# A grouped-query layer whose four input products run in three float32r passes, and whose turned rows are split by ScalarE and VectorE

## The reference

```python
q = x @ Wq                       # 256 -> 256
k = x @ Wk                       # 256 -> 64: four groups of heads share keys
v = x @ Wv                       # 256 -> 64
q = _rope(q, cos, sin); k = _rope(k, cosk, sink)
p = softmax(q @ k.T / sqrt(D));  o = (p @ v) @ Wo
# feed-forward on the same x, 64 slots
ctx = concatenate([x, slot_mean])
h = gelu(ctx @ w1.T + b1)
route_logits = (h @ w2.T + b2) / (abs(tau) + 0.1)
# top 8 of 64, softmax: alpha; slot_input = alpha.T @ x; a GRU step; out = alpha @ slot_values
```

## Time and profile before

| what | value |
|---|---|
| median of 3 runs | 3073.55 us (3070.24 to 3075.05) |
| profiled execution | 3092.09 us, span 3090.4 us |
| mean granted clock of TensorE | 0.956 of full speed |
| PEld (weight loads) | 1805.8 us, 58% |
| ACT (ScalarE) | 1387.8 us, 45% |
| POOL (GpSimd) | 394.5 us, 13% |

### The profile page before, as it was taken

The page is one execution under the profiler, slowest core; times in us unless marked ns, Lnnn a source line. Parts: engine busy times, 40 slices in busy tenths (PEclk is TensorE's granted clock), DMA queues, the critical chain, the costliest instruction groups (busy, mean ns, idle before and its releaser), DMA issues.

```text
span 3090.4 us, 53706 instructions
## 1 busy us (share of the span) xinstructions
PE 2780.4 (90%) x15686; PEld 1805.8 (58%) x15687; DVE 1868.2 (60%) x4512; ACT 1387.8 (45%) x2011; POOL 394.5 (13%) x373
## 2 busy tenths in 40 slices
PE   4999999999988888888879999999899579999998
PEld 2566556546644444443437777776666356666666
DVE  5666666666637777777737677772122456566653
ACT  1644554454433555555545455432233144444443
POOL 1011001100100000000021211221111312222220
PEclk7999999999987999999999999999999789999999
DMA  6534543654412122221214111122311233333330
GB/s 193 166 119 139 171 140 104 180 152 138 119 39 88 56 70 70 70 69 56 70 51 166 46 36 54 48 89 71 109 62 60 89 98 105 103 102 102 101 98 16
DMA packets 157951, 294.55 MB, mean 95 GB/s; under 512 B 24928, under 2 KB 82657, under 8 KB 149057
## 3 DMA queue, kind: packets, MB, share of 16 engines
q1 hardware_dynamic: 145264, 259.59, 27.8%
q0 software_dynamic: 10464, 28.59, 3.0%
q10 hardware_dynamic: 2160, 5.61, 0.5%
HBM read 194.02 MB, written 99.68 MB: 95 GB/s over the span
## 4 chain that ended last, share of the span: by engine, by line
PE 69%; DVE 12%; DMA 6%; issue 6%; ACT 4%; SPq 2%; DVEq 0%; another core or an unknown queue 0%; POOL 0%; ACTq 0%; POOLq 0%
PE bank_u L573 6%; PE pair L557 5%; PE pair L616 4%; PE bank L1984 4%; PE pair L733 4%; PE pair L2134 4%; DVE nmax L910 3%; PE pair L3074 3%; PE pair L777 3%; PE bank_m L3038 3%; PE bank L534 3%; PE bank L3038 3%; PE bank L2589 3%; PE pair L1482 2%; DMA k_a<-parts_dram 2%
## 5 line engine op out<-in xcount | busy, mean ns | idle before, releaser
L816 ACT ACTIVATE probs<-pair 128x1024 f32<-128x1024 f32 x512 | 502.1, 1021 | 218.7 <-PE pair L557 217.9
L910 DVE TENSOR_REDUCE nmax<-bank 128x1 f32<-128x512 f32 x664 | 441.8, 685 | 175.1 <-PE bank L534 127.0
L910 DVE TENSOR_REDUCE nmax<-bank_m 128x1 f32<-128x512 f32 x360 | 246.5, 685 | 106.7 <-PE bank_m L534 59.8
L573 PE MATMUL bank_u<-probs,vext 128*32 128x512 f32 x2048 | 288.7, 637 | 0.6 <-ACT uraw L803 0.5
L557 PE MATMUL pair<-q_a,k_a 98*128 98x512 f32 x512 | 176.4, 450 | 22.2 <-ACT probs L816 11.8
L534 PE MATMUL bank<-k_a,q_a 96*128 96x512 f32 x336 | 149.3, 479 | 27.4 <-DMA k_a<-parts_dram 24.0
L2282 DVE CUSTOM_DVE_ANT_0 bank<-bank,mask_q 128x128 f32<-128x128 f32 (+1 forms) x320 | 118.8, 420 | 89.5 <-PE bank_m L2024 67.1
L557 PEld LDWEIGHTS pair<-q_a,k_a 98*128 98x128 f32 x512 | 90.3, 202 | 122.0 <-ACT probs L816 66.4
L797 ACT ACTIVATE mrow<-bank 8x512 f32<-8x512 f32 x87 | 50.2, 577 | 231.1 <-PE bank L543 231.1
L2134 PE MATMUL pair<-fc,hid 128*128 128x256 f32 x512 | 133.2, 399 | 6.3 <-ACT probs L2175 6.3
L1455 PE MATMUL bank<-k,q 62*128 62x512 f32 x302 | 113.2, 478 | 26.7 <-DVE nmax L910 26.7
(11 more groups left out here) (471 smaller groups left out, 6036.9 us busy)
## 6 DMA issues: line engine op xcount, KB each, us to landing
parts_dram<-parts SPq DMA_DIRECT2D x64, 512.0 KB
q<-parts_dram SPq DMA_DIRECT2D x126, 128.0 KB
q_a<-parts_dram SPq DMA_DIRECT2D x31, 512.0 KB
k_a<-parts_dram SPq DMA_DIRECT2D x31, 512.0 KB
xs<-xres SPq DMA_DIRECT2D x24, 512.0 KB, 3.1
xl<-xs SPq DMA_DIRECT2D x24, 512.0 KB, 3.9
x_in<-xg SPq DMA_DIRECT2D x74, 128.0 KB, 2.1
yg_dram<-y_out POOLq DMA_DIRECT2D x72, 128.0 KB, 2.0
```

The costliest lines, as they stand in the source:

```text
L573: ins = nc.tensor.matmul(bank_u[32 * h:32 * h + 32, :], vext[:, kt, kv(g, h), :], probs[:, kt % 2, h * SEQ:(h + 1) * SEQ], start=(kt == 0) ...
L816: nc.scalar.activation(probs[:, kt % 2, hp * 2 * SEQ:hp * 2 * SEQ + n], st.tile(l, name)[:, 0:n], ACT.Exp).then_inc(st.free["act"].sem, 1)
L910: nc.vector.tensor_reduce(nmax[:, g % 2, qt, h:h + 1], sc.tile(l, name)[:], AX, ALU.max, negate=True).then_inc(sc.free["dve"].sem, 1)
```

## The change

1. The four weights of the products, Wq, Wk, w1's part for x and Wv, are split once into a high and a low part, by GpSimd behind POST0 (`pool_split1`: four copies, four subtractions). TensorE waits for the eight instructions ahead of PRE1.
2. ScalarE's copy of T becomes `act_turned_high` into `xnT_high1`, in the same place. VectorE gets `dve_turned_low`, which subtracts it from T and so frees T; in the plan T's reader is now VectorE. It stands behind maximum 13 of group 2 and before 14.
3. `project` takes three float32r passes of two feature blocks, six matmuls a half; the first two passes wait for the high part, the third for the low one. `pe_values` is replaced by `values`, with 24 matmuls of 64 columns.
4. Buffers: `xnT_high1` and the split weights are new; the whole weights lie where the low parts and others do in turn; `spare_q` shrinks. GpSimd waits for V of POST1 before it splits weights for a later layer.

```diff
 def st_plan1(front, back):
-    return parts_of(front, back, ("back", [("V", "dve")] + e_uses(0, 0, 2)), ("front", [("T", "act")]),
+    return parts_of(front, back, ("back", [("V", "dve")] + e_uses(0, 0, 2)), ("front", [("T", "dve")]),
...
-        turned_high = sig("turned_high", [(1, 0), 0, 0, 0], "scalar")
+        turned_high = sig("turned_high", [(1, 0), (1, 0), 0, 0], "scalar")
...
-        def act_turned_high(act, l, it):
+        def act_turned_high(act, l, it, high):
             act.wait_ge(*st.filled(l, it, "T"))
-            nc.scalar.activation(xnT_high0[:, :, :].rearrange("p k n -> p (k n)").bitcast(F32R), st.tile(l, "T")[:],
+            nc.scalar.activation(high[:, :, :].rearrange("p k n -> p (k n)").bitcast(F32R), st.tile(l, "T")[:],
                                  ACT.Copy).then_inc(turned_high.sem, 1)
...
+        def dve_turned_low(dve, l, it, high):
+            dve.wait_ge(*turned_high.at(l, it, 1))
+            nc.vector.tensor_tensor(xnT_low[:, :, :].rearrange("p k n -> p (k n)").bitcast(F32R), st.tile(l, "T")[:],
+                                    high[:, :, :].rearrange("p k n -> p (k n)"), ALU.subtract).then_inc(st.free["dve"].sem, 1)
...
-            def project(name, half, weight, width=P, halves=2):
+            def project(name, half, high, low, width=P, halves=2, before_low=lambda: None):
...
-                for k_ in range(KT):
-                    ins = nc.tensor.matmul(st.tile(l, name)[0:width, half * SEQ:(half + 1) * SEQ], weight[:, k_, :], xnT[:, k_, :],
-                                           start=(k_ == 0), stop=(k_ == KT - 1))
+                for n, (weight, turned) in enumerate(((high, xnT_high1), (low, xnT_high1), (high, xnT_low))):
+                    if n == 2:
+                        before_low()
+                    for k_ in range(KT):
+                        ins = nc.tensor.matmul(st.tile(l, name)[0:width, half * SEQ:(half + 1) * SEQ],
+                                               weight[:, k_, :].bitcast(F32R), turned[:, k_, :].bitcast(F32R),
+                                               start=(n == 0 and k_ == 0), stop=(n == 2 and k_ == KT - 1))
...
-                pe_values(pe, l, it, wv1)
+                values()
...
+            def values():
+                for s in st.vacated(l, it, "V"):
+                    pe.wait_ge(*s)
+                for t in range(TT):
+                    at = slice(t * P, (t + 1) * P)
+                    for n, (turned, weight) in enumerate(((xnT_high1, wv1_high), (xnT_high1, wv1_low), (xnT_low, wv1_high))):
+                        for k_ in range(KT):
+                            ins = nc.tensor.matmul(st.tile(l, "V")[:, t * DIM:t * DIM + 64], turned[:, k_, at].bitcast(F32R),
+                                                   weight[:, k_, :].bitcast(F32R),
+                                                   start=(n == 0 and k_ == 0), stop=(n == 2 and k_ == KT - 1))
+                ins.then_inc(st.full.sem, 1)
...
+            def turned_parts():
+                pe.wait_ge(*done(st, l, it, "T"))
...
                 if front and g == 0:
-                    pe.wait_ge(*done(st, l, it, "T"))
-                    project("QQ", 0, wq1[:, :, 0:P])
+                    pe.wait_ge(*turned_high.at(l, it, 1))
+                    project("QQ", 0, wq1_high[:, :, 0:P], wq1_low[:, :, 0:P], before_low=turned_parts)
...
                     if front and g == 0 and kt == 1:
-                        act_copy_xnT(act, l, it)
+                        act_turned_high(act, l, it, xnT_high1)
...
-                maxima(2, 10, 16)
+                maxima(2, 10, 14)
+            if front:
+                dve_turned_low(dve, l, it, xnT_high1)
             if back:
+                maxima(2, 14, 16)
                 maxima(3, 0, 2)
...
+        def pool_split1(pool):
+            parts1 = ((wq1, wq1_high, wq1_low), (wk1, wk1_high, wk1_low), (w1x, w1x_high, w1x_low), (wv1, wv1_high, wv1_low))
+            pool.wait_ge(loaded1, N1)
+            pool.wait_ge(*st.filled(POST0, 0, ("E", GROUPS - 1, TT - 1, 1)))
+            for w, high, low in parts1:
+                nc.gpsimd.tensor_copy(high[:].bitcast(F32R), w[:]).then_inc(weights1_split, 1)
+            pool.wait_ge(weights1_split, 4)
+            for w, high, low in parts1:
+                nc.gpsimd.tensor_tensor(low[:].bitcast(F32R), w[:], high[:], ALU.subtract).then_inc(weights1_split, 1)
...
             pool0(pool, POST0, 0, step)
+            pool_split1(pool)
...
             pool1(pool, POST1, 0, step)
+            pool.wait_ge(*st.filled(POST1, 0, "V"))
             pool_split_weights(pool)
...
             pe.wait_ge(dve_set1, 5)
+            pe.wait_ge(weights1_split, 8)
             pe1(pe, PRE1, 0)
```

More of the change, by code:

```diff
@@ L843, in early @@
                 if kt == 2 and front:
-                    act_turned_high(act, l, it)
+                    act_turned_high(act, l, it, xnT_high0)
             def first_max(kt):
@@ L976, in dve0 @@
             if front:
-                dve.wait_ge(*turned_high.at(l, it, 1))
-                nc.vector.tensor_tensor(xnT_low[:, :, :].rearrange("p k n -> p (k n)").bitcast(F32R), st.tile(l, "T")[:],
-                                        xnT_high0[:, :, :].rearrange("p k n -> p (k n)"), ALU.subtract).then_inc(st.free["dve"].sem, 1)
+                dve_turned_low(dve, l, it, xnT_high0)
             maxima(3, 6, 12)
@@ L1263, in build @@
         q_1 = sb("q_1", [P, GROUPS, GH // 2, SEQ], F32, l1)
-        spare_q = sb("spare_q", [P, 8 * SEQ], F32, l1)
+        xnT_high1 = sb("xnT_high1", [P, KT, SEQ], F32, l1)
+        wq1_high = sb("wq1_high", [P, KT, DIM], F32, l1)
+        wk1_high = sb("wk1_high", [P, KT, 2, 64], F32, l1)
+        w1x_high = sb("w1x_high", [P, KT, P], F32, l1)
+        wv1_high = sb("wv1_high", [P, KT, 64], F32, l1)
+        spare_q = sb("spare_q", [P, 1920], F32, l1)
         k_1 = sb("k_1", [P, GROUPS, SEQ], F32, l1)
@@ L1277, in build @@
         sin1 = sb("sin1", [P, SEQ], F32, l1)
-        wq1 = sb("wq1", [P, KT, DIM], F32, l1)
+        whole_wq1 = ExitStack()
+        wq1 = sb("wq1", [P, KT, DIM], F32, whole_wq1)
+        whole_wq1.close()
+        wq1_low = sb("wq1_low", [P, KT, DIM], F32, l1)
         wos = sb("wos", [P, KT, DIM], F32, l1)
@@ L1282, in build @@
         turn_k = sb("turn_k", [64, 2, SEQ], F32, l1)
-        w1x = sb("w1x", [P, KT, P], F32, l1)
+        whole_w1x = ExitStack()
+        w1x = sb("w1x", [P, KT, P], F32, whole_w1x)
+        whole_w1x.close()
+        w1x_low = sb("w1x_low", [P, KT, P], F32, l1)
         w1s = sb("w1s", [P, KT, P], F32, l1)
-        wk1 = sb("wk1", [P, KT, 2, 64], F32, l1)
-        wv1 = sb("wv1", [P, KT, 64], F32, l1)
+        whole_wk1 = ExitStack()
+        wk1 = sb("wk1", [P, KT, 2, 64], F32, whole_wk1)
+        whole_wk1.close()
+        wk1_low = sb("wk1_low", [P, KT, 2, 64], F32, l1)
+        whole_wv1 = ExitStack()
+        wv1 = sb("wv1", [P, KT, 64], F32, whole_wv1)
+        whole_wv1.close()
+        wv1_low = sb("wv1_low", [P, KT, 64], F32, l1)
         slots = sb("slots", [64, DIM], F32, l1)
@@ L1540, in pe1 @@
                 if front and g == 0:
[L1541 to L1542 removed]
+                    pe.wait_ge(*turned_high.at(l, it, 1))
+                    project("QQ", 0, wq1_high[:, :, 0:P], wq1_low[:, :, 0:P], before_low=turned_parts)
                     last_maxima(0, 2)
[L1544 removed]
+                    project("QQ", 1, wq1_high[:, :, P:2 * P], wq1_low[:, :, P:2 * P])
                     last_maxima(2, 4)
[L1546 to L1548 removed]
+                    project("KK", 0, wk1_high[:, :, 0, :], wk1_low[:, :, 0, :], 64)
+                    project("KK", 1, wk1_high[:, :, 1, :], wk1_low[:, :, 1, :], 64)
+                    project("H", 0, w1x_high, w1x_low, P, 1)
                     last_maxima(4, 6)
```

6 lines of the change are left out of this document (1 added, 5 removed).

## The result

The changed kernel takes 3120.0 us (median of four runs, 3115.6 to 3121.3) where the kernel before takes 3074.3 (four runs, 3070.2 to 3086.0). The medians' quotient is 1.0149; the ratio over the fast runs is 1.0135, 95% interval 1.0118 to 1.0152, and a repeat gave 1.0136 (e15). The forecast was 3097.6, its upper end 3110. The direction was right and the size was not: 46 us by the medians, 41.5 by the ratio, instead of 24. The profiled execution took 3120.55, its span is 3118.8.

What follows compares the result with a forecast made beforehand. Bound: a hand-over between nearly full TensorE and VectorE, VectorE late behind the keys. Seven rounds at 2.36 make 16.5, values +8.0, first round -0.5: +24.0 us, 3116.1 in a profile, 3097.6 as median; range 3081 to 3110.

Steps and rivals of the forecast that it cites:

- Step 1: Query product in layer 1's rounds: each half goes from 1.92 to 1.38 us in float32r; -1.08 us a round.
- Step 2: Key and slot products: 5.49 us become 4.14, but only VectorE's wait counts; -0.36 us a round.
- Step 3: T's pair, freed by VectorE's subtraction behind two maxima, holds up TensorE's second score pair of key tile 2; +2.10 a round.
- Step 4: Value product: 16 matmul records become 24; +0.91 us a round, +1.74 in two half-clock rounds, +8.0 in sum.
- Step 5: TensorE's wait at T, grown from 0.44 to 2.5 us, brings the clock to 1.2 GHz; +1.7 us a round.
- The term for the first round: Layer 1's first round: first half waits for the subtraction, but halves save 1.08; -0.5 us.
- the weight splitting: GpSimd, behind POST0's last score pair: about 4.5 us with the casts, hidden by POST0's output product.
- number 2: Rival: second clock fall, at TensorE's 1.5 us wait for the keys' pair; 3104.6, longer falls 3109.5; chance 0.22, both forms.
- Number 3: Rival: quick weight loads for the values, 24 matmuls in 1.37 instead of 2.74 us; 3085.5; chance 0.07.
- Number 1: Rival: no fall of the clock behind the longer wait at T; +12.1, 3085.7; chance 0.17.
- Number 4: Rival: TensorE's own sum decides, the subtraction hiding behind scores and VectorE having room; 3064; chance 0.05.
- number 5: Rival: VectorE's chain closes up, or quick loads without a clock fall; within 0.2% of no change; chance 0.07.

Runs made afterwards that it cites:

- e15: The changed kernel run again without modification, beside the shifted run on the same chip; 1.0136 of the kernel before.
- e7: Changed kernel with values as one float32 product of 16 records and T freed by ScalarE's copy, leaving float32r projections and VectorE's subtraction; 0.9996 of before.
- e12: Changed kernel with the value product as 12 float32 products, 24 records, as long as the float32r ones; 1.0077 of before.
- e14: Changed kernel with seven more float32r matmuls of 512 columns once, in the layer's first round, shifting the loop in time; 1.0143 of before.
- e16: Changed kernel with its 24 value matmuls 256 instead of 64 columns wide, query weights standing in for value weights; 1.0075 of before.
- e2: Changed kernel with the value product as one float32 product of the high parts, 16 records; 3087.4 us, 1.0047 of before.
- e4: Changed kernel with six more float32r matmuls of 512 columns in TensorE's 1.43 us wait ahead of the values; 3106.3 us, 1.0118 of before.
- e3: Changed kernel with query, key and slot products as float32 products of the high parts, still waiting for T's release; 3138.7 us, 1.0216 of before.
- e9: Kernel before with three more float32 matmuls of 256 columns, some 1.4 us, ahead of each query product; 1.0045 of before.
- e5: Changed kernel with VectorE's subtraction moved two maxima earlier, behind maximum 11, so the stall at T was 1.71 us; 1.0136 of before.
- e1: Changed kernel with T freed by ScalarE's copy and VectorE's low part taken from that copy, so no stall; 3088.7 us, 1.0051 of before.
- e6: Changed kernel with float32 query, key and slot products and T freed by ScalarE's copy, keeping 24 short value matmuls and VectorE's subtraction; 1.0121 of before.
- e8: Changed kernel with four more float32r matmuls of 512 columns, some 0.9 us, ahead of each query product; 1.0147 of before.
- e13: Kernel before with float32r query, key and slot products, GpSimd making both parts, its wait for last loads behind the first round; 0.9998 of before.

## Why the prediction was off, step by step

- **Step 1, query halves:** a term a little too large. 1.60 a half instead of 1.38; the first pass behind another product and the last ahead of one take 0.58 and 0.56, not 0.46. Layer 0's row stood for the middle of a chain. -0.63 a round instead of -1.08.
- **Step 2, keys and slots:** 4.32 instead of 4.14, and the first pair of group 1 came 0.75 earlier instead of 0.36, as its wait was 0.97, not 1.5. Steps 1 and 2 together -1.38 against the -1.44 of the sum. The step failed behind that point: it asked which wait comes last up to 1163.60 and not what is late next. ScalarE's chain from the summed queries over the gelu to the parts of the keys was, first at the score pair 0.72 us behind the last row; it comes earlier only by step 1's 0.63. Worth of both steps at the round's end: 0.66 (e7). Error: 7 x 0.78 = 5.5 us.
- **Step 3, the release of T:** right. 2.51 for "about 2.5", +2.09 for +2.10.
- **Step 4, values:** their own time right, 2.70 for 2.74, and 7.4 us more over the seven rounds for 8.0. The reading of before had a slip: one of its seven rounds begins at the low clock, at 966.65, and in the one at 1381.51 the clock falls 1.3 us in, so its 16 records take 2.35 and not 3.47. What the short products do to the clock was not thought of.
- **Step 5, the clock:** the step that failed. It put one fall of 1.7 us into each round, behind the stall. Measured are 5.0 a round (88.7 against 83.7 of e12), in the traced execution 3.45 of it behind the values and some 1.6 behind group 1's first pair, and none at the stall. Its evidence, seven falls at seven long waits (the first 1.8 us behind the wait's end and not within 1.5), had two weak sides. The five waits of 1.6 to 2.8 us were all in layer 0. And it went from waits to falls and never from falls to waits: between 80 and 900 us the same trace has 15 falls, ten of them with no wait over 1.1 us in the 10 us before. So a long wait was not needed for a fall. One of the ten, with TensorE busy 4.21 of the 5 us before (columns as in the earlier trace rows):

```profile
848.50:853.50 5.00, 4.21 (x13) 2.01 (x11) 3.92 (x7) 1.94 (x2) 0.00 (x0) 1.00 0.70 253
854.00:863.50 9.50, 9.24 (x29) 3.29 (x29) 5.57 (x10) 4.74 (x6) 0.00 (x0) 0.50 0.37 68
```

  In layer 1 the same stall of 2.5 us was followed by a fall in none of seven rounds (after, e15, e12), in four (e14) or in six (e16). Over the loop the clock cost 25.6 more than before (41.7 less 7 x 2.3 of work); the forecast had 11.9 in step 5 and 1.7 in step 4. It was 12 us short.
- **The base:** in the loop 41.7 us were measured for the 24.5 of the forecast (24.0 and PRE1's 0.5), a difference of 17.2: 12 of clock and 5.5 of work, less 0.3 by which values and stall were cheaper. The ratio's 41.5 us (interval 36 to 47) agrees with that; the medians' 46 is 4 more. The term for the first round, -0.5, came as -0.2 (from its first projection to the loop, 44.04 us for 44.25), and the weight splitting is hidden, as forecast. On the profiled execution the sum said 3116.1, and 3120.55 came, which looks like a hit. It misses by 4 where the median misses by 22, and that is chance: the profiled execution of before was 13 us longer than that of after in layers that the change leaves alone. An excess of a profile over the median should first be looked for by stage.
- **The rivals:** number 2 (a second fall) came nearest with 3104.6, and with 3109.5 in its longer form; a second fall there was in the traced execution, at the place it named or just behind, but on top of a first one elsewhere. Number 3 (quick weight loads) fell: 2.70 us for 24 loads is 0.112 apiece, as in float32 (0.114). The Trainium skill, "TensorE: Matmul & The Clock Gate", section "Weight-path perf modes — Fast Weight Load (FWL) and DoubleRow", names float32 as the one type that is left out of the quickening; in this kernel float32r isn't quickened either, by this row. Number 1 (no fall) is what e2's and e12's free rounds show to be possible, 82.8 and 83.7. Number 4 fell with the stall of 2.51 us, number 5 with the time.

The Trainium skill, same page, section "Why this matters for your kernels", ties drops of the clock to idle time between matmuls. The longest waits agree: in the trace of before the clock is low within those of 7.20 and 7.83 us. But e16 against the changed kernel has the same wait of 1.43 us and the same 24 loads, and differs only in the columns (and in which weights they come from): 0 of 7 against 7 of 7 falls. So waits are not all there is to count: 24 narrow float32r matmuls, paced by their weight loads, brought the clock down where wide ones did not, and with the wait filled (e4) they did so in 3 of 7.

**What stays open.** Why e3, e9 and e5 end where they do isn't settled: dense work added can lengthen a round by more than itself, and a shorter stall can bring nothing. The runs show that the place in time matters for the falls other than those behind the values, not a rule by which to compute it. How the narrow values and the pattern of later falls share the 5.0 us a round isn't separated: e15 has the same round with one longer fall.

## What to carry to other kernels

Before moving a product from float32 to three float32r passes, look at its columns: with 64 of them the passes are paced by weight loads, save nothing (2.70 against 1.83 us), and can bring TensorE's clock down for the 10 us that follow, which here cost four times as much as the work (3.45 against 0.87 us a round). Before taking falls for the work of long waits, list every fall of the trace, those without a long wait too. Price the clock by the round and not by the wait: compare a round without a fall with the mean of all. And a saving is worth what the next late engine leaves of it: follow it to the end of the round, not to the first wait that shrinks.

## What the runs showed of the hardware that was not expected

- The granted clock fell with TensorE busy in all of the 3 us before (1148 to 1151, then 0.51 for 10.5 us).
- 24 float32r matmuls of 64 columns behind a wait of 1.43 us: a fall in 7 of 7 rounds in each of seven runs (after, e15, e14, e1, e3, e5, e6), in 6 of 7 with dense work added elsewhere (e8). 24 float32 records of the same columns and length: 2 of 7. 24 float32r of 256 columns: 0 of 7. The narrow float32r ones with the wait filled (e4): 3 of 7.
- A stall of 2.51 us was met by a fall in 0 to 7 of 7 rounds, in kernels that have the same stall (after 0, e14 4, e16 6, e3 7).
- The layers behind layer 1, which no run changed, took 1449 to 1474 us, grouped by chip (1449 to 1451 on one, 1470 to 1474 on another).
- GpSimd casts 128 x 1024 float32 to float32r in 1.04 us and subtracts in 2.4, both beside VectorE's maxima. The timeline of e13:

```profile
1223.32 1.04 POOL L1903 CAST xnT_high<-xnT 128x1024 fp32r<-128x1024 f32 x1
1224.44 2.44 POOL L1905 TENSOR_TENSOR xnT_low<-xnT,xnT_high 128x1024 fp32r<-128x1024 f32 x1
```
